# Two more chunks of a top-k search in four steps instead of three, and what follows them a step later

## What is computed

```python
x = x + L1_attn(layernorm(x), ...)              # 16 heads of 64, causal softmax, projected out
x = x + L1_xattn(layernorm(x), ctx, ...)        # 16 heads of 8 over 77 context rows:
    # scores = Q K^T / SCALE
    # topk_scores, topk_indices = top_k(scores, 32)
    # context = sum of softmax(topk_scores) * V[topk_indices]; then Wo, bo
x = x + L1_ffn(layernorm(x), ...)               # 8 experts of 512, the two best of each token
    # h = relu(x Wg^T) * (x Wu^T); out = sum over the two of weight * (h Wd^T)
```

## Time and profile before

| | |
|---|---|
| median of 3 runs | 611.92 us (611.89 to 613.57) |
| the profiled execution | 608.84 us, its span 607.1 us |
| PE busy | 535.3 us (88%) |
| DVE busy | 411.4 us (68%) |
| ACT busy | 293.7 us (48%) |
| POOL busy | 223.1 us (37%) |
| the chain that ended last | PE 56%, DVE 23%, ACT 8%, issue 7%, POOL 4% |

### The profile page before, as it was taken

How to read it: one execution, slowest core, us unless ns; L and a number is a source line. 1 busy time by engine, 2 the same in 40 slices (tenths; PEclk the granted TensorE clock), 3 DMA queues, 4 the chain that set the end, 5 groups by cost and what they waited for, 6 DMA issues and landing times.

```text
span 607.1 us, 12163 instructions
## 1 busy us (share of the span) xinstructions
PE 535.3 (88%) x3982; PEld 421.5 (69%) x3982; DVE 411.4 (68%) x2225; ACT 293.7 (48%) x726; POOL 223.1 (37%) x227
## 2 busy tenths in 40 slices
PE   4888779996999899989999879969889999899997
PEld 2565347874666566768678656668667778899997
DVE  3666865543534598776698998974967798744543
ACT  2334213326765566674763646543774655222221
POOL 5016820003433364563553655550634433340000
PEclk9999799999999999999988989986999999899999
DMA  4600102404000000000000000001520000010000
GB/s 127 188 1 15 53 14 76 150 1 157 3 1 1 0 2 2 2 1 3 1 2 1 2 3 2 1 1 53 192 65 6 18 15 19 18 33 1 27 1 10
DMA packets 23050, 19.17 MB, mean 32 GB/s; under 512 B 2048, under 2 KB 18508, under 8 KB 22989
## 3 DMA queue, kind: packets, MB, share of 16 engines
q1 hardware_dynamic: 22477, 17.36, 9.4%
q0 software_dynamic: 512, 1.05, 0.6%
HBM read 15.38 MB, written 3.01 MB: 30 GB/s over the span
## 4 chain that ended last, share of the span: by engine, by line
PE 56%; DVE 23%; ACT 8%; issue 7%; POOL 4%; DMA 1%; DVEq 0%; POOLq 0%; ACTq 0%
PE ps L1793 48%; DVE wk L1165 5%; PE ps L2183 4%; DVE top L1155 3%; DVE nmax L1101 3%; ACT w_mem L1555 2%; DVE sel_mem L994 1%; ACT prT L1562 1%; PE ps L2245 1%; POOL xs_dram L770 1%; DVE bn L825 1%; DVE xn L838 1%; DVE sel_mem L1289 1%; DVE xn L1128 1%; PE ps L1805 1%
## 5 line engine op out<-in xcount | busy, mean ns | idle before, releaser
L1165 DVE MATCH_REPLACE8 wk<-top,wk 128x77 f32<-128x77 f32 x384 | 80.5, 224 | 0.0
L1101 DVE TENSOR_REDUCE nmax<-ps 128x2 f32<-128x256 f32 (+1 forms) x64 | 51.2, 820 | 37.7 <-PE ps L1793 35.8
L687 POOL TENSOR_TENSOR w_mem<-w_mem,rinv 128x256 f32<-128x256 f32 (+3 forms) x44 | 53.1, 1218 | 51.4 <-DVE rinv L1107 50.8
L1289 DVE TENSOR_TENSOR sel_mem<-gr,ps 128x512 f32<-128x512 f32 x47 | 32.2, 686 | 48.8 <-ACT gr L1736 48.0
L1155 DVE MAX8 top<-wk 128x8 f32<-128x77 f32 x384 | 58.0, 223 | 0.0
L1736 ACT ACTIVATE gr<-ps 128x512 f32<-128x512 f32 x47 | 28.0, 596 | 61.0 <-PE ps L1793 61.0
L1793 PE MATMUL ps<-cat_mem 64*128 64x512 f32 (+7 forms) x272 | 53.1, 470 | 1.5 <-ACT cat_mem L1539 1.5
L1555 ACT ACTIVATE w_mem<-ps,nmax 128x128 f32<-128x128 f32 (+3 forms) x88 | 44.4, 519 | 12.0 <-DVE nmax L1101 11.9
L716 POOL TENSOR_SCALAR wk<-wk 128x616 f32<-128x616 f32 x16 | 28.0, 1753 | 56.6 <-DVEq L1169 56.2
L1793 PE MATMUL ps<-prT,cat_mem 128*64 128x128 f32 x640 | 44.0, 286 | 1.8 <-DVE x L1190 1.3
L611 POOL TENSOR_TENSOR rstd<-var_eps,minus_half 128x4 f32<-128x4 f32 x8 | 8.2, 1025 | 95.0 <-DVE var_eps L831 94.9
(11 more groups left out here) (346 smaller groups left out, 1371.0 us busy)
## 6 DMA issues: line engine op xcount, KB each, us to landing
w_mem<-in_L_ffn_W_dram SPq DMA_DIRECT2D x12, 256.0 KB, 3.1
f_mem<-in_L_ffn_Wg_dram SPq DMA_DIRECT2D x8, 256.0 KB, 2.7
f_mem<-in_L_ffn_Wu_dram SPq DMA_DIRECT2D x8, 256.0 KB, 3.1
f_mem<-in_L_ffn_Wd_dram SPq DMA_DIRECT2D x8, 256.0 KB, 3.9
sel_mem<-in_L_ffn_W_dram SPq DMA_DIRECT2D x4, 256.0 KB, 4.7
xs_dram<-zero SPq DMA_DIRECT2D x1, 960.0 KB, 6.1
ys_dram<-f_mem SPq DMA_DIRECT2D x15, 64.0 KB, 1.5
xs<-xs_dram SPq DMA_DIRECT2D x3, 256.0 KB, 3.4
```

The costliest lines, as they stand in the source:

```text
L687: pool.tensor_tensor(pr[s][:, :, at:at + n], pr[s][:, :, at:at + n], rinv[:, i % 8, :].unsqueeze(2).to_broadcast([P, 2, n]), ALU.mult)\
L1101: dve.tensor_reduce(nmax[:, i % 8, :], ps[:, 2 * s:2 * s + 2, at:at + (c + 1) * P], X, ALU.max, negate=True).then_inc(nmax_ready, 1)
L1165: dve.match_replace(wk[q][:, t, h, :], top[q][:, t, h, 8 * r:8 * r + 8], src[:, t, h, :], GONE).then_inc(top_step, 1)
L1289: dve.tensor_tensor(hg[s][:, :], gr[s][:, :], ps[:, 2 * s + 1, :], ALU.mult)\
```

## The change

Chunks 8 and 9 are searched in four units each, 41 to 44 and 45 to 48; as there is no unit 48, the fourth round of chunk 9 is step 0 of the last stage. The double steps end with chunk 7. piece_late is shifted by one, so chunk 10 begins at step 1, and everything of blocks 2 and 3 that follows from the search stands one j or i later in the lists of POOL, DVE, ACT and PE. On DVE, gate(13) and shares_of(1) change places: before, shares_of stood between gate(12) and gate(13), and now it stands between gate(13) and gate(14). No instruction is added or taken away.

```diff
--- before.py
+++ after.py
@@ -63,8 +63,10 @@
 
     if 12 <= U < 28:
         return divmod(U - 12, 4)
-    if 29 <= U < 47:
+    if 29 <= U < 41:
         return 4 + (U - 29) // 3, (U - 29) % 3
+    if 41 <= U < 48:
+        return 8 + (U - 41) // 4, (U - 41) % 4
     return None, None
 
 
@@ -75,12 +77,12 @@
 def double_step(U):
 
     n, r = piece_of(U) if 0 <= U < NU else (0, None)
-    return r == 2 and n >= 4
+    return r == 2 and 4 <= n < 8
 
 
 def piece_late(step):
 
-    return divmod(40 + step, 4) if step <= 26 else (None, None)
+    return divmod(39 + step, 4) if step <= 27 else (None, None)
 
 
 class Count:
@@ -797,17 +799,17 @@
                     add_bo(3)
             places_lo(0)
             for j in range(NS):
-                if j == 6:
+                if j == 7:
                     rstd_two(2, gn_var, gn_rstd)
                 cross(E + j)
                 if j in (1, 5, 9):
                     places_lo((j + 3) // 4)
-                if j == 9:
+                if j == 10:
                     tokens_lo(2)
             for i in range(2 * E):
-                if i == 7:
+                if i == 8:
                     rstd_two(3, gn_var, gn_rstd)
-                if i == 10:
+                if i == 11:
                     tokens_lo(3)
                 cross(E + NS + i)
                 if i == 2:
@@ -1371,31 +1373,32 @@
             for j in range(NS):
                 if j != 13:
                     gate(j)
-                if j == 3:
+                if j == 4:
                     context_norm(2)
-                if j == 5:
+                if j == 6:
                     add_context(2, ps[:, 4, 0:2 * P])
-                if j == 6:
+                if j == 7:
                     apply_two(2, gn_rstd, gn_ready)
-                if j == 10:
+                if j == 11:
                     gates(1, 4, 2, 4)
                 if j == 12:
+                    gate(13)
+                if j == 13:
                     shares_of(1, 4, 2)
-                    gate(13)
                 cross(E + j)
             for i in range(4 * E):
                 gate(NS + i)
                 if i % 2 == 0 and i:
                     combine(i // 2 - 1)
-                if i == 4:
+                if i == 5:
                     context_norm(3)
-                if i == 6:
+                if i == 7:
                     add_context(3, ps[:, 4, 0:2 * P])
-                if i == 7:
+                if i == 8:
                     apply_two(3, gn_rstd, gn_ready)
-                if i == 11:
+                if i == 12:
                     gates(2, 6, 2, 4)
-                if i == 13:
+                if i == 14:
                     shares_of(2, 6, 2)
                 if i in (14, 15):
                     add_sparse(i - 14)
@@ -1762,13 +1765,13 @@
                 if j:
                     evac_y(j - 1)
                 cross_two(E + j)
-                if j == 3:
+                if j == 4:
                     evac_cn(2, four)
-                if j == 7:
+                if j == 8:
                     norm_two(2, gnT_ps, gnT_ready, four)
-                if j == 9:
+                if j == 10:
                     tokens_hi(2)
-                if j == 10:
+                if j == 11:
                     gates(1, 4, 2)
             for i in range(4 * E):
                 if i:
@@ -1777,13 +1780,13 @@
                 if i == 0:
                     evac_y(NS - 1)
                 cross_two(E + NS + i)
-                if i == 4:
+                if i == 5:
                     evac_cn(3, four)
-                if i == 8:
+                if i == 9:
                     norm_two(3, gnT_ps, gnT_ready, four)
-                if i == 9:
+                if i == 10:
                     tokens_hi(3)
-                if i == 11:
+                if i == 12:
                     gates(2, 6, 2)
 
 
@@ -2562,13 +2565,13 @@
                 if j:
                     down_rows(j - 1)
                 four = cross_two(E + j, *four)
-                if j == 3:
+                if j == 4:
                     four = context_T(2, out_x, *four)
-                if j == 4:
+                if j == 5:
                     four = project_context(2, out_x, *four)
-                if j == 7:
+                if j == 8:
                     four = norm_two(2, gn_ready, gnT_ps, gnT_ready, out_x, *four)
-                if j == 9:
+                if j == 10:
                     route(2, 4, 2, 4, *four)
                     four = ((lg_ready, 3),)
             down_rows(NS - 1)
@@ -2578,13 +2581,13 @@
                 four = cross_one(E + NS + i, *four)
                 down(i)
                 four = cross_two(E + NS + i, *four)
-                if i == 4:
+                if i == 5:
                     four = context_T(3, out_x, *four)
-                if i == 5:
+                if i == 6:
                     four = project_context(3, out_x, *four)
-                if i == 8:
+                if i == 9:
                     four = norm_two(3, gn_ready, gnT_ps, gnT_ready, out_x, *four)
-                if i == 10:
+                if i == 11:
                     route(3, 6, 2, 4, *four)
```

## The result

The changed kernel takes 619.5 us (median of 6 runs, 613.6 to 622.7); the kernel before takes 611.2 in the runs beside it (607.7 to 613.6). The ratio is 1.012, with a 95% interval of 1.008 to 1.016, so +7.3 us (+4.8 to +9.8); the two medians as they stand are 8.3 us apart. Ratios leave out the few executions that ran over 1.5% above their kernel's fastest, medians hold them. It is slower, as forecast, and by somewhat more than the +5.1 of the forecast. The profiled execution has a span of 620.0 us.

What follows compares the result with a forecast made beforehand. Bound by chunk 8's double step delaying unit 46's maximum, then PE's work list at a lowered clock, with PE full from 520 us. Terms -1.5 + 0 + 3.8 + 1.0 + 1.2 + 0.6 = +5.1 gave 617.0 us, range 609.5 to 621.0.

Steps and rivals of the forecast that it cites:

- Units 43 to 47: Search units without the double steps of chunks 8 and 9: values(31) starts earlier, -1.5 us, bounds -0.5 to -3.7.
- b = 1: Last stage, step 1: ACT's scores copy for chunk 11 waits for chunk 9's last round behind the places, +3.8 us.
- The clock in that wait: PE's pause of about 4 us in b = 1 drops its granted clock: +1.0 us, between 0 and +2.5.
- b = 2 to 7: Later steps of the last stage: a chunk's weights, two transposes, come in here, +1.2 us, bounds -1.5 to +2.5.
- rival (b): Slack in b = 2 to 7 absorbs the wait and weights: +1.1 us, 613.0, within 0.3%; chance 0.18.
- The row tiles: The 15 row tiles: gate(14) 0.6 us earlier, but chunk 14's weights behind it: +0.6 net, bounds -2 to +3.
- The column steps: The 32 column steps: block 3's context normalised a step later, users with about five steps of room, cost 0.
- The clock behind gate(14): PE's lower clock after its wait for gate(14): growth counted only in the row tiles' upper bound of +3.
- Rival (a): PE's clock stays high through b = 0, saving 5.1 us: -1.5 in all, 610.4, faster; chance 0.16.
- Rival (c): The tail worsens: wait for gate(14) doubles, lower clock covers it and b = 2: +9.0, 620.9; chance 0.12.

Runs made afterwards that it cites:

- e0: The changed kernel run again, unchanged, as the measure for the others: 618.6 us, ratio 1.010 to the kernel before.
- e12: Changed kernel plus 17 matmuls without a user in PE's wait in b = 1 only: 619.6 us, ratio 1.011 to the kernel before.
- e6: Changed kernel plus matmuls without a user, 17 in the b = 1 wait and 23 ahead of hidden_T(14): 615.6 us, ratio 1.005.
- e3: Changed kernel with shares_of back ahead of gate(13) and chunk 9's last round taken early, where DVE idled: 611.8 us, ratio 1.001.
- e8: As e3, with POOL masking and picking chunk 9 in b = 0 ahead of rstd_two(3): 611.8 us, ratio 1.001.
- e9: As e8, with DVE's add_sparse in column steps 15 and 17 instead of 14 and 15: 609.5 us, ratio 0.997.
- e1: Changed kernel with only shares_of of block 2 put back ahead of gate(13): 614.8 us, ratio 1.006.
- e2: Changed kernel with only chunk 9's last round moved ahead of the last attention block's copy, where DVE idled: 617.0 us, ratio 1.009.
- e10: As e5, plus matmuls without a user: 4 ahead of values(31), 9 ahead of hidden_T(14): 605.1 us, ratio 0.989.
- e5: Kernel before with chunk 8 in four single steps and chunk 9 a unit later, double step in unit 47, nothing moved behind: 610.7 us, ratio 0.996.
- e11: e5 run again, unchanged: 608.7 us, ratio 0.995 to the kernel before.
- e4: Kernel before with only shares_of of block 2 moved behind gate(13), one step later: 612.3 us, ratio 1.001.

## Why the prediction was nearly right, and where not

The direction, the range and the main term were right. Term by term, with what the runs showed in its place:

- **Units 43 to 47, -1.5 forecast.** The working holds to a tenth up to the maximum of unit 47. PE's values(31) starts 2.6 us earlier than before in e0 and 1.0 earlier in the profile after, on the common clock. Between the two lies one stretch of lower clock over values(30), as in the kernel before, which e0 does not have. On the way, apply_two met a POOL operation, the condition that the forecast gave for its bound of -0.5; that cost DVE 0.5 us, and PE did not wait for it.
- **b = 1, +3.8.** Measured 4.75 - 1.19 = +3.56, and ACT, PE and POOL are released as told.
- **The clock in that wait, +1.0.** e12 to e0: 0.4 us; e12 to the profile after: 1.5. Inside its bounds.
- **b = 2 to 7, +1.2.** Mis-sized: -0.3. With the clock at 1.00 (e6, e12) they take 30.2 us, against 30.53 before. The two transposes of the weights find room. So a part of rival (b) is true. The runs without the wait (e3, e8, e9) need 31.17 to 31.19, with a stretch of lower clock in them; whether that is the clock alone, or also rounds and picks that got ahead during the wait, is not settled. e1 to e8 puts the net price of the wait, with POOL's order mended, at some 3 us (3.0 by the medians, 3.2 by the ratios, with 3 to either side).
- **The row tiles, gate(14) 0.6 earlier.** This is the step that failed in its reading of the trace. It comes 1.6 later (62.53 against 60.95). I took the block on shares_of to go, since at its new place it would meet the one-input L716. It meets the pick behind that (L1284, 1.26 us instead of 0.17). That is 1.1 of the 2.2 us that were missed (over the 2 us that the forecast had set as a sign of being wrong); the other 1.1 lies in gate(13), only 2.0 us earlier from gate(0) than before (52.7 against 54.8), and in the waits between the two rounds, and is not separated further. Order and block together are 62.52 - 60.34 = 2.2 us (e2 to e8), and 64.12 - 61.95 = 2.2 (e0 to e1). In e0, e6 and e12 gate(14) is 3.2 later than before, not 1.6: the rest is the lower clock in the row tiles, which the forecast has nowhere. (The Trainium skill, "SBUF — State Buffer", Terms, says that the loser of the shared port waits for a full instruction of the other; L1284 and the two L1183 end with POOL's operation, 0.03 us after it in the one case and 0.34 in the other, and so the trace agrees. In e3 it agrees for L1319, 0.03 us after the pick; the three cum are through 0.85 us before the mask is over and are held for 0.45 us only, so there the trace does not agree with a wait for the full instruction.)
- **The column steps, +1.2 for the weights, in the 0.6.** The largest miss. With the clock at 1.00 in both, the kernel after needs 85.89 (e6) where e10 needs 81.91: +4.0. PE is busy 82.44 against 81.11 us, which is the weights of chunk 14; the other 2.7 are pauses that the kernel before does not have: 0.58, 0.56 and 1.00 us, the last from shares_of and add_sparse in one step (e9 takes it back), and 0.5 more left ahead of hidden_T(14) itself. What brings the first two is not tested. "Its users have five steps of room" was true and beside the point: the cost came from what stood together in DVE's step, not from who waited for the result.
- **The clock behind gate(14), 0 forecast in the likeliest case.** It is low for longer than before in the profile after, in e0 and in e12. The column steps of e10, before and e5, whose instructions are the same, take 81.91, 83.57 and 85.20: 3.3 us between none and the most of lower clock. The same 2.27 us pause ahead of it gave the middle one once and the worst one twice.
- **Rival (a)** had its mechanism right and its consequence wrong. Its sign, tile_id before 421, showed up in the profile after: 420.5 on the old clock. The clock did stay up in b = 0 in one of five profiles. From values(31) to tile_id it took 17.63 us before, 17.64 in e0 and 13.09 in the profile after: 4.55 us saved, near the 5.1. The stretch of lower clock over values(30) cost 1.6 of it in the same profile. What was wrong is the premise that nothing else would take it: tile_id came 5.5 us early by the common clock, and the tail gave up more.
- **Rival (c)** had 0.12, too little. Its mechanism at gate(14), a wait twice as long and the lower clock behind it, came true: 5.82 us instead of 2.27, and a mean granted clock of 0.69 in the 9 us behind. The measured +7.3 lies between the forecast's +5.1 and its +9.0, and nearer to (c)'s.

The sum for the profile after, from the maximum of unit 45: -0.5 - 5.0 + 3.6 + 1.0 + 1.6 + 4.6 = +5.2. That this is nearly the forecast's 5.1 is chance: 4 us more gain up to tile_id and 1.5 less cost from there to gate(0) stand against 5.6 more in the tail. In e0, with the clock low in b = 0, the same sum is -0.5 - 2.1 + 3.6 - 0.1 + 3.2 + 5.0 = +9.1. Over the runs it is +7.3. That in most of them the clock in b = 0 is low, as in four of five profiles, is likely but not shown for executions without a profile.

What stays open is what decides, in an execution, whether the clock falls over values(30) or behind values(31). The pause ahead of values(31) was 0.93 us in e0 (low) and 0.93 in after, e5 and e11 (high). The two go together: of the twelve profiles with the changed units, seven have the lower clock over values(30) and then high in b = 0 (after, e2, e8, e9, e5, e11, e10), five the other way round; before and e4 have it in both places. With the stretch in the row tiles it is the same five. Why is open.

## What to carry to other kernels

When all that follows moves a step later, count each step of the later order anew as a sum for its engine, with its neighbours on the other engine that share a port: here two things that used to stand in different steps and now stand in one cost 1.0 us (add_sparse beside shares_of) and 2.2 us (shares_of between two rounds, with POOL's pick over it), and the round that came to stand behind the places 3.6. A step of PE's work that leaves a stretch in which PE waits, and lands in one in which PE is full, costs its whole length there and gives back little where it was. Take the part of such a change that gains (here the units) without the shift that pays for it, and price a pause of PE with the slower stretch behind it: nine matmuls without a user ahead of gate(14) belonged to a version that is 6.6 us faster than the kernel before.

## What I had not expected of the hardware

The same instructions take different times from execution to execution by the clock of PE alone. At the maximum of unit 45 the profile after was 7.7 us behind that of before with nothing changed up to there. Over the fourteen profiles the maximum of unit 47 starts between 392.98 and 401.38 us, of which the change makes 0.5. Yet where such stretches lie alike the times repeat to 0.02 us: 27.01, 27.01, 27.02 to tile_id in e5, e11 and e10.

A 2.27 us pause of PE was followed by 9 us at a mean granted clock of 0.62 in e5; with 9 matmuls of some 0.22 us in the pause, which left 0.24 us of it, the same 9 us ran at 1.00. And a pause is not needed: in e0 the clock fell in the row tiles when PE had been busy 6.32 of 6.46 us and then all of 1.78 us with matmuls of 9 columns; after, with the same instructions and the same busy time, kept 1.00.
